# Four edits around the convolutions of a one-core network: who adds up, who splits, when offsets are turned and where group statistics are taken

## The chip, the cores and the metric

The kernel runs on one core of one Trainium2 chip. The metric is the device time of one launch in microseconds (us). Before the change the median of three runs is 1823.61 us (1823.13 to 1826.45).

## The reference

A network of four blocks works on `x` of shape (8, 64, 32, 32) in float32. Every block is `x = x + conv(ln(x))`, then on tokens `t = t + ffn(ln(t))`. The parts that matter here, shortened:

```python
# conv 0: batch norm over all images, then linear attention
mean, var = x.mean(axis=(0, 2, 3)), x.var(axis=(0, 2, 3))
xn = (x - mean) * rsqrt(var + 1e-5) * bn_gamma + bn_beta
k, q, v = wk @ xn + bk, wq @ xn + bq, wv @ xn + bv          # softmax of k over pixels, of q over channels
# conv 1: a 3x3 kernel of its own for each image, mixed out of 8 experts
gap = x.mean((2, 3)); cw = relu(gap @ w1.T) @ w2.T
pooled = x.reshape(b, c, 4, 8, 4, 8).mean((3, 5))            # 16 cells of 8x8 pixels
routing = sigmoid(cw[:, :, None] * (pooled.mean(1).reshape(b, 16) @ w_exp.T)[:, None, :])
combined = einsum('bik,koiuv->boiuv', routing, weight)
# conv 3: deformable convolution, then group norm (32 groups) and relu
offset = conv3x3(x, offset_w) + offset_b                     # 18 offsets a pixel
out = deform_conv(x, offset, deform_w)                       # bilinear samples at 9 shifted places
g = out.reshape(b, 32, -1); out = relu((g - mean(g)) * rsqrt(var(g) + 1e-5) * gamma + beta)
```

The four feed-forward parts are mixtures of experts with the two best experts of each token; the change leaves them alone.

## The kernel before

The activations `x` and their normalised copy `xn` stay in SBUF as 128 partitions (2 halves of the batch times 64 channels) by 4096 columns (4 images of 1024 pixels). The program is a chain of stages: a layer norm, a convolution, a layer norm, a mixture, four times over. Each stage is written by hand as one instruction list for each engine, joined by counting semaphores, so an engine does its instructions in written order and waits where the text says so. Engines run from one stage to the next without a barrier, except around the sampling of conv 3, where a `Block` of its own ends: there all engines meet.

The names that the change touches:

- `split_weights` (GpSimd) cuts the first weights of the next mixture into a rounded part `w_high` (copies, L456) and a rest `w_low` (subtractions, L460), 512 columns at a time; only the next mixture needs them. It is called in conv 0, 1, 2 and in `offsets`.
- `batch_norm` (conv 0): VectorE joins the statistics, TensorE averages the two halves (L1189), VectorE and ScalarE work out scale and shift in operations of one column (L1215 to L1222), and VectorE scales `xn` image by image (L1225, semaphore `bn.scaled`). TensorE multiplies by the key weights (L962) as each image is there. Meanwhile `keep_awake` (L54) gives TensorE products into a bank that nobody reads.
- `conv1`: VectorE sums `xn` in runs of 8 pixels (`row_sum`, L1320), then over 8 rows (`cells`, L1321), then to one total an image (L1323). Small products on TensorE (L1288 to L1291) and a sigmoid give the routing; VectorE mixes one kernel an image (L1337 to L1342), and TensorE convolves (L1301).
- `offsets` (conv 3): TensorE makes the offsets in two rounds `r` of two images each (L1630, 64x32 tiles, 8 at a time side by side), ScalarE adds the bias (`off`, L1616), TensorE turns them (L1638), VectorE copies them to `coords` (L1661) and looks for the largest (L1665 to L1673). The result `flag` says whether any offset leaves the near window.
- `sample_near`: the near samples as a pipeline over items; VectorE multiplies hat weights (`weigh`, L1866), TensorE turns (L1737) and multiplies (L1766) them, `keep` (L1872) takes half an image of results to `y`.
- `sample_rest`: the far samples, all under a condition. Each engine loads `flag` (L1930) and branches (L1931). With these inputs the flag is 0 and the body is skipped. It has a block of its own, so a barrier (L1912) ends it.
- `group_norm`: eight `bn_stats` over `y` (L2118), then a chain of small operations, a product (L2094) and the affine part.

## Time and profile before

| | |
|---|---|
| median of three runs | 1823.61 us |
| time of the profiled execution | 1823.78 us |
| span of its trace | 1822.0 us |
| TensorE busy | 1684.6 us (92%) |
| VectorE busy | 1083.1 us (59%) |
| ScalarE busy | 975.4 us (54%) |
| GpSimd busy | 870.1 us (48%) |
| mean granted clock of TensorE | 0.97 |

The shares are averages over very different stages. The four mixtures fill most of the span and keep TensorE busy; in the pieces between them one engine after the other is alone on the path. In the rows below, the first two numbers of a timeline row are the start and the length in us, PE is TensorE, PEld its weight loads, DVE VectorE, ACT ScalarE, POOL GpSimd, and a name with q at its end is an engine's sequencer.

### The profile page before, as it was taken

The page shows a single profiled execution, that of the slowest core. Times are in us where ns is not written, and L with a number is a line of the kernel's source. Part 1 is how long each engine was busy: PE and PEld are TensorE (multiplying, and loading weights), DVE is VectorE, ACT ScalarE, POOL GpSimd, SP SyncE. Part 2 cuts the span into 40 slices and gives each one's busy share as a digit, 9 for nine tenths or more (in the row PEclk, how much of TensorE's full clock was granted, in tenths as well). Part 3 has the DMA queues.
Part 4 walks back from the last instruction along what each step waited for, and adds up shares of the span by engine and source line. Part 5 has one row for each costly group of instructions (what it writes and reads, how often), then busy time and mean ns, then how long its engine had stood idle before and what let it go on. Part 6 is the DMA issues. An engine that isn't in the chain of part 4 may idle for free. (4 is left out here: it accounts for less than half of the span.)

```text
span 1822.0 us, 32613 instructions
## 1 busy us (share of the span) xinstructions
PE 1684.6 (92%) x12391; PEld 962.3 (53%) x12391; DVE 1083.1 (59%) x1532; ACT 975.4 (54%) x1427; POOL 870.1 (48%) x730
## 2 busy tenths in 40 slices
PE   6879999999589999998999997999999769999998
PEld 3744555555244444444444445777777535555554
DVE  6666777766874342365334236656657467777766
ACT  2444555555336666626666645666666355555554
POOL 3318777777024333313333335333323018777777
PEclk8989999999799999999999998999999889999999
DMA  5004333333302222301222240000000003333333
GB/s 125 1 10 110 107 106 110 107 109 99 91 1 77 89 79 70 88 17 33 90 79 71 88 96 1 2 1 2 1 1 1 3 18 113 110 117 115 113 113 104
DMA packets 71588, 121.64 MB, mean 67 GB/s; under 512 B 16962, under 2 KB 18562, under 8 KB 70786
## 3 DMA queue, kind: packets, MB, share of 16 engines
q1 hardware_dynamic: 71426, 119.47, 23.1%
q8 instruction: 103, 1.69, 0.4%
q14 instruction: 59, 0.48, 0.1%
HBM read 115.74 MB, written 3.67 MB: 66 GB/s over the span
## 5 line engine op out<-in xcount | busy, mean ns | idle before, releaser
L747 POOL TENSOR_TENSOR x<-x,mx_gated 128x512 f32<-128x512 f32 x254 | 327.2, 1288 | 97.4 <-DVE mx_gated L699 96.1
L692 DVE TENSOR_TENSOR mx_hidden<-ps,mx_hidden 128x1024 f32<-128x1024 f32 (+1 forms) x256 | 246.1, 961 | 181.6 <-PE ps L560 181.6
L560 PE MATMUL ps<-tokens_high,w_high 64*128 64x512 f32 x1536 | 331.3, 427 | 13.6 <-DVE mx_hidden L692 6.6
L855 ACT ACTIVATE mx_hidden<-ps,w_bias 128x1024 f32<-128x1024 f32 x256 | 264.2, 1114 | 121.3 <-PE ps L560 121.3
L560 PE MATMUL ps<-tokens_low,w_high 64*128 64x512 f32 x1536 | 306.7, 395 | 0.0
L560 PE MATMUL ps<-tokens_high,w_low 64*128 64x512 f32 x1536 | 306.5, 395 | 0.0
L901 POOL TENSOR_TENSOR x<-x,mx_gated 128x512 f32<-128x512 f32 x126 | 161.4, 1281 | 256.4 <-DVE mx_gated L873 256.4
L873 DVE SCALAR_TENSOR_TENSOR mx_gated<-ps,w_bias,mx_gates 128x512 f32<-128x512 f32 x128 | 96.0, 750 | 283.2 <-PE ps L825 266.3
L675 ACT ACTIVATE mx_hidden<-ps 128x1024 f32<-128x1024 f32 x256 | 248.5, 1022 | 15.9 <-PE ps L560 1.9
L629 PE MATMUL ps<-mx_hidden,w_second 128*64 128x512 f32 x1024 | 249.3, 605 | 4.8 <-DVE mx_hidden L692 3.4
L1866 DVE TENSOR_TENSOR c_near_weights<-c_near_hats 128x768 f32<-128x768 f32 x192 | 190.1, 1037 | 103.3 <-PE ps L1737 103.2
L560 PEld LDWEIGHTS ps<-tokens_high,w_high 64*128 64x128 f32 x1536 | 146.2, 186 | 189.8 <-DVE mx_hidden L692 95.1
L825 PE MATMUL ps<-mx_hidden,w_second 128*64 128x512 f32 x1024 | 233.4, 598 | 0.0
L667 ACT COPY mx_kept<-ps 128x512 f32<-128x512 f32 x126 | 74.0, 587 | 263.0 <-PE ps L560 263.0
L740 POOL TENSOR_TENSOR mx_hidden<-mx_kept,mx_hidden 128x512 f32<-128x512 f32 x126 | 172.6, 1370 | 67.8 <-ACT mx_kept L667 67.8
L699 DVE TENSOR_TENSOR mx_gated<-ps,mx_gates 128x512 f32<-128x512 f32 x256 | 172.3, 685 | 7.0 <-PE ps L629 6.9
L560 PEld LDWEIGHTS ps<-tokens_high,w_low 64*128 64x128 f32 x1536 | 146.1, 186 | 34.4
L560 PEld LDWEIGHTS ps<-tokens_low,w_high 64*128 64x128 f32 x1536 | 146.7, 187 | 23.4
L1844 POOL TENSOR_TENSOR c_near_dist<-c_near_position,c_ints 128x288 f32<-128x288 f32 x64 | 65.1, 1018 | 194.7 <-DVE c_near_hats L1856 191.3
L1815 ACT COPY c_near_matrix<-ps 128x512 f32<-128x512 f32 x288 | 149.1, 608 | 8.5 <-PE ps L1737 8.4
L1737 PE MATMUL ps<-identity,c_near_weights 128*128 128x128 f32 x1152 | 138.7, 278 | 0.0
L825 PEld LDWEIGHTS ps<-mx_hidden,w_second 128*64 128x64 f32 x1024 | 68.0, 136 | 133.6 <-issue 115.3
(222 smaller groups left out, 1830.5 us busy)
## 6 DMA issues: line engine op xcount, KB each, us to landing
mx_gates<-gate_board SPq DMA_DIRECT2D x768, 128.0 KB, 3.1
w_first<-in_f_first SPq DMA_DIRECT2D x4, 1024.0 KB, 12.0
c_weight<-in_c_weight SPq DMA_DIRECT2D x1, 2304.0 KB
x<-in_x SPq DMA_DIRECT2D x8, 256.0 KB, 5.3
w_second<-in_f_second SPq DMA_DIRECT2D x4, 512.0 KB, 13.3
w_first<-in_f_first SPq DMA_DIRECT2D x4, 512.0 KB, 10.1
out_x<-x SPq DMA_DIRECT2D x16, 128.0 KB, 2.7
gate_board<-xn SPq DMA_DIRECT2D x16, 64.0 KB, 2.8
```

The source lines that it names most:

```text
L560: last = pe.matmul(out[h], weights[w][half(h), w_own], tokens[t][half(h), t_own], start=(p == 0), stop=(p == 2))
L629: last = pe.matmul(out[half(h), slot(n), :], w.second[:, e * C:(e + 1) * C], hidden[:, n % HIDDEN, h, :], start=True, stop=True)
L675: act.activation(hidden[:, n % HIDDEN], first[:, n % FIRST], ACT.Silu).then_inc(s.act.semaphore, 1)
L692: dve.tensor_tensor(own, second[:, 0:halves, :], own, ALU.mult).then_inc(s.hidden.semaphore, 1)
L699: dve.tensor_tensor(gated[:, n % GATED, :], out[:, slot(n), :], gates.spread[:, n % gates.SLOTS, :], ALU.mult).then_inc(s.gated.semaphore, 1)
L740: pool.tensor_tensor(own, kept[:, m // 2 % KEPT, :], own, ALU.mult).then_inc(s.other.semaphore, 1)
L747: pool.tensor_tensor(place, place, gated[:, n % GATED, :], ALU.add).then_inc(s.added.semaphore, 1)
L825: last = pe.matmul(out[half(h), slot(n), :], w.second[:, (e * F + f) * C:(e * F + f + 1) * C], hidden[:, n % HIDDEN, f, h, :], start=(f == ...
L855: act.activation(hidden[:, n % HIDDEN, f], first[:, (n * F + f) % BLOCKS], ACT.Gelu, bias=w.bias1[:, e * F + f:e * F + f + 1]).then_inc(s. ...
L901: pool.tensor_tensor(place, place, gated[:, n % GATED, :], ALU.add).then_inc(s.added.semaphore, 1)
L1815: act.copy(own, turned[:, c % BANKS, :].rearrange("p (h b c) -> p h b c", h=HALVES, c=P)).then_inc(s.matrix, 1)
L1866: dve.tensor_tensor(weights[:, u % SLOTS].rearrange("p t (r c) -> p t r c", c=W), spread(own[:, :, W:W + ROWS], 3, W), spread(own[:, :, 0: ...
```

## The change

1. `split_weights` takes a function that is called between its two loops; in conv 0 it waits until all four images are scaled, so that the subtractions come behind the batch norm. `keep_awake` there does 2 products, not 4.
2. In conv 1 GpSimd sums the cells of the first two images (`ON_GPSIMD`) by halving, in six additions an image; VectorE sums the other two and then waits for GpSimd's. `keep_awake` with 12 products is new behind the small products.
3. In `offsets` the first round's offsets are turned amid the second round's products, and their largest and smallest are found before the second round's.
4. The `bn_stats` of the group norm move into `sample_near`, two places behind each `keep`. Each engine loads `flag` there too. The body of `sample_rest` and the group norm stand in one block, so the barrier between them is gone; where the far samples are taken, the statistics are taken again.

```diff
-def split_weights(k, pool):
+def split_weights(k, pool, between=None):
...
         pool.tensor_copy(w.high[:, own], w.first[:, own]).then_inc(k.gt.w_high, 1)
+    if between:
+        between()
     for own in pieces:
...
-            split_weights(k, pool)
+            split_weights(k, pool, lambda: pool.wait_ge(k.bn.scaled, IMAGES))
...
-        keep_awake(k, pe, awake, 4)
+        keep_awake(k, pe, awake, 2)
...
             pool.memset(padded[:], 0.0).then_inc(s.cleared, 1)
+            for j in range(ON_GPSIMD):
+                pool.wait_ge(k.ln.normed, normed + 2 * (j + 1))
+                folded = pixels_of(j, j + 1)
+                for i, width in enumerate((CELL // 2, CELL // 4, CELL // 8)):
+                    to = partial[:, i, 0:H * POOL * width] if width > 1 else rows_of(j, j + 1)
+                    to = to.rearrange("p (n x) -> p n x", x=width)
+                    pool.tensor_tensor(to, folded[:, :, 0:width], folded[:, :, width:2 * width],
+                                       ALU.add).then_inc(s.pool_rows, 1)
+                    pool.wait_ge(s.pool_rows, 5 * j + i + 1)
+                    folded = to
...
+                for i, height in enumerate((CELL // 2, CELL // 4, CELL // 8)):
...
+                    pool.tensor_tensor(to, folded[:, :, 0:height, :], folded[:, :, height:2 * height, :],
+                                       ALU.add).then_inc(s.pool_cells if height == 1 else s.pool_rows, 1)
...
             pe.matmul(tiny[:, 64:128], average[:], cells[:], start=True, stop=True).then_inc(s.small_ps, 1)
+            keep_awake(k, pe, ps[0][:, 0, :], 12)
...
-            done(dve.tensor_reduce(row_sum[:], xn[:].rearrange("p (n x) -> p n x", x=CELL), AX.X, ALU.add))
-            done(dve.tensor_reduce(cells[:].rearrange("p (j q) -> p j q", q=POOL),
-                                   row_sum[:].rearrange("p (j y q) -> p j q y", y=CELL, q=POOL), AX.X, ALU.add))
+            done(dve.tensor_reduce(rows_of(ON_GPSIMD, IMAGES), pixels_of(ON_GPSIMD, IMAGES), AX.X, ALU.add))
+            done(dve.tensor_reduce(cells_of(ON_GPSIMD, IMAGES), cell_rows_of(ON_GPSIMD, IMAGES), AX.X, ALU.add))
+            dve.wait_ge(s.pool_cells, ON_GPSIMD)
...
+        TURN_AT = 4
...
                 for t in range(TAPS):
+                    if r == 1 and t in (TURN_AT, TURN_AT + 1):
+                        turn(0, t - TURN_AT)
...
-            dve.tensor_reduce(reach[:, 0:1], rows, AX.XY, ALU.max)
-            done(dve.tensor_reduce(reach[:, 1:2], rows, AX.XY, ALU.min))
-            dve.scalar_tensor_tensor(out=reach[:, 2:3], in0=reach[:, 1:2], scalar=-1.0, in1=reach[:, 0:1],
-                                     op0=ALU.mult, op1=ALU.max).then_inc(s.reach, 1)
+            done(dve.scalar_tensor_tensor(out=reach[:, 4:6], in0=reach[:, 2:4], scalar=-1.0, in1=reach[:, 0:2],
+                                          op0=ALU.mult, op1=ALU.max))
+            dve.tensor_tensor(reach[:, 6:7], reach[:, 4:5], reach[:, 5:6], ALU.max).then_inc(s.reach, 1)
...
+                if g == 1 and ty == 6:
+                    statistics(j, 0)
+                if g == 1 and ty == 1 and j >= 1:
+                    statistics(j - 1, 1)
                 for h in range(HALVES):
                     weigh(n, h)
...
+            look(dve)
             keep(IMAGES - 1, 1)
-            dve.wait_ge(s.kept, 2 * IMAGES)
+            statistics(IMAGES - 1, 1)
+            dve.wait_ge(s.stats, 2 * IMAGES)
...
-        block = ctx.enter_context(nc.Block(no_gpsimd_drain=True))
+        block = k.block
...
-            for g in range(N // BANK):
-                last = dve.bn_stats(stats[:, g, :], y[:, g * BANK:(g + 1) * BANK])
-            done(last)
```

Three places in the built program show what moves. First GpSimd in conv 0, with the semaphores that each instruction waits for: the copies and subtractions of `split_weights`, then the softmax of the queries. Before:

```order
6 L456 CAST w_high<-w_first 128x512 [waits w_loaded]
7 L456 CAST w_high<-w_first 128x512 x7
8 L460 ISA
9 L460 TENSOR_TENSOR w_low<-w_first,w_high 128x512 [waits gt_w_high] x8
10 L1040 TENSOR_TENSOR c_qv<-c_qv,c_q_max 128x8x128 [waits c0_q_max] x4
```

and of the change:

```order
6 L456 CAST w_high<-w_first 128x512 [waits w_loaded]
7 L456 CAST w_high<-w_first 128x512 x7
8 L462 ISA
9 L462 TENSOR_TENSOR w_low<-w_first,w_high 128x512 [waits gt_w_high,bn_scaled]
10 L462 TENSOR_TENSOR w_low<-w_first,w_high 128x512 [waits gt_w_high] x7
11 L1042 TENSOR_TENSOR c_qv<-c_qv,c_q_max 128x8x128 [waits c0_q_max] x4
```

The order is the same; the first subtraction now also waits for `bn_scaled`. Second, TensorE in `offsets`, the products of the offset convolution and the transposes of `off`. Before:

```order
1844 L1630 MATMUL ps<-c_padded,c_w_off 32x512 x144
1845 L1638 MATMUL ps<-identity,c_off 128x128 x16
1846 L1642 MATMUL ps<-identity,c_reach 1x128
```

and of the change:

```order
1845 L1676 MATMUL ps<-c_padded,c_w_off 32x512 x104
1846 L1661 MATMUL ps<-identity,c_off 128x128 x4
1847 L1676 MATMUL ps<-c_padded,c_w_off 32x512 x8
1848 L1661 MATMUL ps<-identity,c_off 128x128 x4
1849 L1676 MATMUL ps<-c_padded,c_w_off 32x512 x32
1850 L1661 MATMUL ps<-identity,c_off 128x128 x8
1851 L1683 MATMUL ps<-identity,c_reach 1x128
```

Eight of the sixteen transposes now stand between products, in two groups of four. Third, VectorE at the end of the sampling: the last multiplications of weights, the last `keep` and the way to the group norm. Before:

```order
787 L1866 TENSOR_TENSOR c_near_weights<-c_near_hats 128x768 x8
788 L1872 COPY c_y<-ps 128x512
789 L1686 UNCONDITIONAL_BRANCH
790 L2014 UNCONDITIONAL_BRANCH
791 L2075 MEMSET c_rest_staged 128x96 x2
792 L1930 TENSOR_LOAD c_flag
793 L1930 ISA x2
794 L1931 COMPARE_AND_BRANCH
```

and of the change:

```order
798 L1918 TENSOR_TENSOR c_near_weights<-c_near_hats 128x768 x8
799 L1746 TENSOR_LOAD c_flag
800 L1746 ISA x2
801 L1924 COPY c_y<-ps 128x512
802 L1929 BN_STATS c_stats<-c_y 128x6
803 L1730 UNCONDITIONAL_BRANCH
804 L2079 UNCONDITIONAL_BRANCH
805 L1991 COMPARE_AND_BRANCH
```

The load of the flag moved ahead of the last copy, one of the statistics stands behind it, and the clearing of the staging buffer left the way to the branch.

## Rows read from the trace of the kernel before

**Rows 1.** The page's costliest groups: busy, mean ns, idle before and its releaser.

```profile
L1866 DVE TENSOR_TENSOR c_near_weights<-c_near_hats 128x768 f32<-128x768 f32 x192 | 190.1, 1037 | 103.3 <-PE ps L1737 103.2
```

**Rows 2.** Timeline of the batch norm (start, length, engine, line, idle before).

```profile
32.40 3.76 PE L54 MATMUL ps<-identity 128*128 128x256 f32 x8
...
33.05 11.62 POOL L460 TENSOR_TENSOR w_low<-w_first,w_high 128x512 fp32r<-128x512 f32 x8
...
33.58 0.75 DVE L1220 TENSOR_TENSOR bn_both<-bn_both,c_cols 128x1 f32<-128x1 f32 x1
...
36.81 6.74 DVE L1225 TENSOR_SCALAR xn<-xn,bn_both 128x1024 f32<-128x1024 f32 x4
38.58 0.50 PEld L962 LDWEIGHTS ps<-xn,c_wk 128*128 128x128 f32 x2 [3.13 <-DVE xn L1225]
...
56.20 1.91 POOL L1040 TENSOR_TENSOR c_qv<-c_qv,c_q_max 128x1024 f32<-128x1024 f32 x1 [11.53 <-DVE c_q_max L1113]
```

**Rows 3.** Timelines elsewhere: two like operations of VectorE with GpSimd idle.

```profile
1458.83 0.16 DVE L2134 TENSOR_TENSOR gn_group<-gn_group 128x4 f32<-128x4 f32 x1
...
481.49 0.52 DVE L1337 TENSOR_SCALAR c_mixed<-c_weight,c_routing 128x576 f32<-128x576 f32 x1 [0.30 <-ACT c_routing L1281]
```

**Rows 4.** Windows (length, busy PE PEld DVE ACT POOL, granted clock, DMA) as the clock rises.

```profile
41.00:42.00 1.00, 1.00 (x2) 0.29 (x1) 1.00 (x2) 0.38 (x1) 1.00 (x2) 0.56 0.00 0
...
492.00:493.00 1.00, 1.00 (x12) 0.30 (x8) 0.96 (x2) 0.00 (x0) 0.00 (x0) 0.78 0.00 0
```

**Rows 5.** Timeline of conv 1.

```profile
462.83 1.28 DVE L159 TENSOR_TENSOR xn<-xn,ps 128x512 f32<-128x512 f32 x2 [0.74 <-ACT xn L131]
...
471.66 4.42 DVE L1320 TENSOR_REDUCE c_row_sum<-xn 128x512 f32<-128x4096 f32 x1
476.11 1.06 DVE L1321 TENSOR_REDUCE c_cells<-c_row_sum 128x64 f32<-128x512 f32 x1
...
478.58 0.69 PE L1291 MATMUL ps<-c_cells,c_average 128*128 128x64 f32 x2
...
488.14 33.24 PE L1301 MATMUL ps<-c_padded,c_kernel 64*64 64x512 f32 x288 [8.87 <-DVE c_kernel L1342]
...
509.27 0.82 DVE L1342 SCALAR_TENSOR_TENSOR c_kernel<-c_weight,c_routing,c_mixed 128x576 f32<-128x576 f32 x1
```

**Rows 6.** GpSimd's two-input operations: page (busy, mean ns) and timeline.

```profile
L747 POOL TENSOR_TENSOR x<-x,mx_gated 128x512 f32<-128x512 f32 x254 | 327.2, 1288 | 97.4 <-DVE mx_gated L699 96.1
...
1171.43 0.32 POOL L1846 TENSOR_TENSOR c_near_dist<-c_near_position,c_ints 128x72 f32<-128x72 f32 x1
```

**Rows 7.** Timeline of `offsets`: the transposes and what follows.

```profile
1094.60 1.30 PEld L1638 LDWEIGHTS ps<-identity,c_off 128*128 128x128 f32 x12 [0.84 <-issue]
...
1097.25 0.75 DVE L1665 TENSOR_REDUCE c_reach<-c_coords 128x1 f32<-128x576 f32 x1
```

**Rows 8.** Timeline of the sampling behind an image's end.

```profile
1206.97 2.29 DVE L1866 TENSOR_TENSOR c_near_weights<-c_near_hats 128x768 f32<-128x768 f32 x2
...
1208.12 2.84 PE L1737 MATMUL ps<-identity,c_near_weights 128*128 128x128 f32 x24
```

**Rows 9.** From the sampling to the group norm: timeline, and sequencer rows by line.

```profile
1444.15 0.69 DVE L1872 COPY c_y<-ps 128x512 f32<-128x512 f32 x1 [11.95 <-PE ps L1766]
...
L1686 PEldq EVENT_SEMAPHORE  x2: 51/51/51, 1444.4 to 1445.3; - x2
...
L1931 PEldq COMPARE_BRANCH  x1: 4090/4090/4090, 1446.3 to 1446.3; - x1
L1931 DVEq COMPARE_BRANCH  x1: 67/67/67, 1446.8 to 1446.8; - x1
...
L1912 DVEq DRAIN  x1: 74/74/74, 1450.0 to 1450.0; - x1
...
1450.96 4.84 DVE L2118 BATCH_NORM_STATS2 gn_stats<-c_y 128x6 f32<-128x512 f32 x8 [4.87 <-PEq L1912]
...
1456.79 0.60 PE L2094 MATMUL ps<-gn_own,c_pairs 128*128 128x8 f32 x2 [12.70 <-DVE gn_own L2126]
```

More of the change, by code:

```diff
@@ L1240, in conv1 @@
     RING = 3
+    ON_GPSIMD = 2
     with ExitStack() as ctx:
@@ L1616, in _, with turn @@
                     act.activation(off[:, r, h, :], ps[r][:, h, :], ACT.Identity, bias=off_b).then_inc(s.off, 1)
+        TURN_AT = 4
         @block.tensor
         def _(pe):
+            def turn(r, h):
+                pe.wait_ge(s.off, HALVES * r + h + 1)
+                for q in range(CHUNK_TILES):
+                    last = pe.transpose(turned[:, r, h, q * P:(q + 1) * P], off[:, r, h, q * P:(q + 1) * P], k.identity[:])
+                last.then_inc(s.turned, 1)
             pe.wait_ge(k.fetched_sem, k.fetched)
@@ L1697, in sample_near, with look @@
         block = ctx.enter_context(nc.Block(no_gpsimd_drain=True))
+        beyond = {}
+        def look(eng):
+            beyond[eng.engine] = eng.value_load(flag[0:1, 0:1], min_val=0, max_val=1)
         def place_of(n):
@@ L1922, in sample_rest, with run @@
         turned, sum_ps = banks(k, 0, 2, TAP_GROUP), banks(k, 2 * TAP_GROUP, 2)
[L1923 to L1927 removed]
+        block = k.block
+        def run(eng, body, prepare=None, conclude=None):
+            with eng.If(beyond[eng.engine] > 0):
+                if prepare:
+                    prepare()
                 with eng.Fori(0, IMAGES, 1) as j:
                     body(j)
[L1930 to L1932 removed]
+                if conclude:
+                    conclude()
         @block.tensor
```

81 lines of the change are left out of this document (54 added, 27 removed).

## The prediction, made before the changed kernel ran

> **What bounds the kernel now.** I read the page first. By the table above TensorE is busy for 92% of the span and VectorE for 59%, so no engine but TensorE can be the bound of the whole. But the change touches none of the mixtures that fill most of that time. It touches four pieces between them, and there the share says nothing: I took the timeline of each piece and asked which operation the next engine's first instruction waits for. In the batch norm it is VectorE's scaling (TensorE's weight load for L962 waited 3.13 us for L1225) [rows 2]. In conv 1 it is VectorE's sums and then its first kernel (8.87 us of TensorE's idle time) [rows 5]. In `offsets` it is TensorE's products and then VectorE's search. At the end of the sampling it is first TensorE, then the branches and the barrier, then VectorE's statistics (L2094 waited 12.70 us) [rows 9]. Inside the sampling TensorE is the pace: VectorE's weights waited 103.2 us for its transposes [rows 1]. All pieces stand one behind another, so what one gains or loses reaches the end. The sum is made against the profiled execution's own 1823.78 us, which is 0.17 us above the median of the three runs.
>
> **1, batch norm: -3.6 us.** VectorE's three one-column operations from L1220 on take from 33.58 to 36.81, 3.23 us, while GpSimd subtracts for 11.62 us beside them [rows 2]. The like operation L2134, with GpSimd idle, took 0.16 us [rows 3], 0.20 with the gap to the next. Three make 0.6, saving 2.6. The first scaling ran from 36.81 until TensorE loaded at 38.58, 1.77 us, and the four took 6.74 [rows 2]. Undisturbed, L1337 with the same operation does 576 columns in 0.52 [rows 3]; scaled to 1024 that is at most 0.92, and with a fixed part of some 0.2 it is 0.77. I take 0.77, saving 1.0; the bound is 0.85. TensorE's key products then start at 35.0. The reduced `keep_awake` makes room for that: eight half-products took 3.76 us [rows 2], so two products end at 34.3; four would end at 36.2 and eat 1.2 of the gain. What moves is hidden: the subtractions start when the fourth image is scaled (35.0 + 3 x 0.7 = 37.1), take 8 x 1.29 by the row of a like size [rows 6] and end at 47.4. GpSimd's next work, L1040, started at 56.20 after 11.53 us of waiting for VectorE [rows 2] and would now start at 52.6, so the cover is 5 us; beyond it each us late is one us on the queries. The copies stay where they are. If GpSimd was not what slowed VectorE, the gain is 0. The unlike lengths of like operations speak against that.
>
> **2, conv 1: -4.85 us.** VectorE's sums of 4.42 and 1.06 us are halved [rows 5]: 2.7 less. For GpSimd I draw a line through 512 columns in 1.29 us and 72 in 0.32 [rows 6]: 0.16 fixed and 0.0022 a column. An image takes 512, 256, 128, 64, 32 and 16 columns: 6 x 0.16 + 1008 x 0.0022 = 3.2 us, and five waits for its own results at 0.1, a guess, give 3.7. The first image is normalised at 464.1 (462.83 + 1.28), so two end at 471.5. VectorE reaches its wait at 471.66 + 2.2 + 0.5 = 474.4 [rows 5]. GpSimd has 2.9 us of room, and may take 5.1 an image.
>
> Against this stands a rule of the Trainium skill (Perfetto Trace Analysis, section Optimizing Scalar/DVE Operations): VectorE and GpSimd share an SBUF read port, so moving work between them might not help. The skill's SBUF — State Buffer, section Who interferes with whom, narrows it: on this chip a reduction never contends, nor does an ordinary operation with one SBUF input, and VectorE's here are of these kinds. The trace shows contention for the two kinds that page names, L1220 with two SBUF inputs and the scaling [rows 2]; it has no reduction of VectorE beside a running GpSimd in conv 1.
>
> The filler products come on TensorE behind L1291, which ended at 479.27 and now ends at 476.6. The first kernel, needed for L1301, comes at 488.14 - 2.7 = 485.4, so they have 8.8 us. At 3.76 / 4 = 0.94 us each they would take 11.3 at the low clock [rows 2]. But the clock rises from its lower level (1.2 GHz) to the upper (2.4 GHz) under work: in the batch norm 3.3 us after L962 began, in conv 1 4.3 us after L1301 began (granted 0.56 and 0.78 in the windows where it rose) [rows 4]. With 4.3 us at the low rate, 4.6 products, and 7.4 at 0.47, the filler takes 7.8 us and ends in time. L1301 then runs at the upper level from its start; its first 4.3 us were at half rate, so 2.15 are saved of 33.24. What remains is 31.1, 7.8 an image. VectorE must keep ahead with the kernels: the last one was there at 510.09 [rows 5], now 507.4, and is needed at 485.4 + 3 x 7.8 = 508.7. That holds, with 1.3 to spare.
>
> **3, offsets: +0.9 us.** This part I expect to lose. TensorE's products set the pace until ScalarE's last bias. The eight transposes of the first round were hidden before: they ran while ScalarE evicted the second. Amid the products they cost their own time: weight loads of twelve take 1.30 [rows 7], so eight 0.87. Each of two changes from the tiled products to whole-array transposes may add a drain: TensorE's loads stood idle 0.84 us ahead of the first transpose, but half of this is the length of the last products themselves [rows 7]. I take 0.15 each, 1.2 in all; the bounds are 0.9 and 2.6 (2 x 0.84 more). VectorE's copies of the second round end as far behind the products as before, since they wait for the same ScalarE and TensorE work. The two reductions over 576 elements, 0.75 each [rows 7], become two over half: with some 0.2 fixed, 0.5 each, so 0.5 less. One more small operation costs 0.2. Net -0.3 against +1.2.
>
> **4, statistics in the sampling: +1.3 us.** Seven `bn_stats` of 0.6 (4.84 / 8) [rows 9], nearly 0.7 with their wait, come into VectorE's list. VectorE waits 103.3 us for TensorE in all there, over 190.1 us of work [rows 1], so a place takes 0.7 for nothing unless it stands in a tight stretch. Those behind the middle of an image I cost at nothing by that. Behind the end of an image the stretch is tight: the weights of L1866 are done at 1209.26, and the second of the two sets that TensorE turns from 1208.12 on is wanted halfway through those 2.84 us, at 1209.54 [rows 8]. With 0.7 more VectorE is 0.4 late there, and TensorE pays it at three image ends. Bounds: 0, and 7 x 0.7 = 4.9.
>
> **4, the way to the group norm: -6.3 us.** Before: the last copy ends at 1444.84, all engines meet and are released at 1445.3, TensorE reaches its branch at 1446.3, which holds it for 4.09 us, VectorE has its branch at 1446.8 and is through at 1450.0, the second barrier opens, statistics start at 1450.96, and L2094 at 1456.79 [rows 9]. After: one `bn_stats` and its wait move the release to 1446.0. There are no flag loads or memsets ahead of the branches. The stall of the branch stays; I have no row that would shorten it. The Trainium skill (Runtime: NRT & Kernel Launch, Instruction fetch mechanics) says that a taken branch to a far target must fetch its page first, which agrees with 4.09 us here. TensorE is through at 1446.1 + 4.1 = 1450.2. VectorE branches at some 1446.3, needs 3.2 and then the small operations from 1455.80 to 1456.79, 1.0: 1450.5. So L2094 starts at 1450.5, 6.3 earlier. Bounds: 5, if a fetch is one us longer, and 7.
>
> **Sum.** -3.6 - 4.85 + 0.9 + 1.3 - 6.3 = -12.6. 1823.78 - 12.6 = 1811.2 for an execution like the profiled one, 1811.0 as a median.
>
> **Rivals.**
> - *The clock in the batch norm rises later.* Before, 3.76 us of filler had not raised it, and now the cover is half as long [rows 2, 4]. If the key products run at the lower level for some 4 us longer, at most half of that is lost: +2. The same in conv 1: if it does not rise under the filler, that ends at 487.9, 2.5 late, and L1301 gains little. Times 1813 to 1815.5. For it: the risings at 3.3 and 4.3 us differ already. The skill's TensorE: Matmul & The Clock Gate, Part 1, has the clock follow recent activity, which is this mechanism. Chance 0.15.
> - *VectorE has no room in the sampling.* All seven statistics cost TensorE 0.7: 1814.8. Against it: the 103.3 us of waiting [rows 1]. Chance 0.1.
> - *Sharing between VectorE and GpSimd helps nothing in conv 1*, by the rule above: the 2.7 fall away, 1813.9. Chance 0.07.
> - *The branch eats the barrier's gain.* Only the statistics' 4.84 less 0.7 are won, not the rest: -4.1, 1813.4. Chance 0.1.
> - *GpSimd's folds are late: slower.* Their inner runs are 4, 2 and 1 elements. L1846 with nine runs took 0.32 [rows 6]; all of it put on the runs, 0.035 each, makes 412 runs an image 14.6 us. Beyond 5.1 an image each further us costs two. From 11.4 on the whole change loses; at 14.6 the time is 1811.2 + 19 = 1830. Against it: L1040 with 32 runs takes 1.91 for twice the columns of L747 in one run [rows 2, 6], so runs cost about nothing. Chance 0.03.
> - *Within 0.2%.* Two or three of the first four together, and the upper bound of the transposes. Chance 0.04.
> - The forecast itself, 0.51.
>
> **How the numbers follow.** 0.2% is 3.6 us, about what a measurement of this kernel can tell from no change. The forecast and the first four rivals are all faster by more: 0.93. Same 0.04, slower 0.03. The range goes down to 1807.5 (0.2 and 0.7 more in parts 1 and 4, no loss in the sampling, 0.3 less in the offsets, and a clock that rises a us or two earlier) and up to 1816.5 (two of the rivals at once).
>
> **What would show it.** Right: the three one-column operations under 0.3 us each, the first scaling under 0.9; key products from 35.0; GpSimd's last fold before 472.0 on the old scale; the convolution's products in under 31.5 us; the group's product less than 6 us behind the last `keep`. Wrong: a wait of VectorE for `pool_cells`; TensorE's filler ending behind the first kernel; transposes amid the products with gaps over 0.5 us; TensorE waiting for weights behind each image's end.

## The result, and the profile after

The changed kernel takes 1812.62 us (median of four runs, 1810.42 to 1815.48) against 1823.86 (1823.13 to 1826.45): ratio 0.9937, 95% interval 0.992 to 0.9954. The forecast was 1811.0 (1807.5 to 1816.5). The profiled execution took 1815.48, the slowest of the four, over a span of 1813.7. So its trace is 8.3 us shorter than the one of before (1822.0), while the medians lie 11.2 apart, and the stages have to say where that comes from.

The page of the changed kernel: TensorE's share, the granted clock by slices, and the row that answers to [rows 1].

```profile
PE 1693.6 (93%) x12411; PEld 968.2 (53%) x12411; DVE 1071.0 (59%) x1533; ACT 975.3 (54%) x1427; POOL 870.0 (48%) x742
...
PEclk8889999999899999999999998999999979999999
...
L1918 DVE TENSOR_TENSOR c_near_weights<-c_near_hats 128x768 f32<-128x768 f32 x192 | 188.3, 1028 | 101.8 <-PE ps L1786 101.8
```

VectorE waits as long for TensorE in the sampling as before, less 1.5 us. TensorE is busy for 9.0 us more in a span 8.3 shorter. This isn't more time at the lower clock: the trace of before has 111.0 us at granted 0.50, this one 101.3. It is mostly the new filler: from VectorE's first sum to the end of conv 1's products TensorE is busy for 40.6 us in place of 34.7, and behind the group's product for another 3.1 more; the other stages nearly cancel.

Batch norm, timeline of the changed kernel, to be held against [rows 2].

```profile
33.19 0.50 PEld L1191 LDWEIGHTS ps<-bn_own,c_halves 128*128 128x128 f32 x2 [7.35 <-DVE bn_own L1214]
...
33.64 2.05 PE L54 MATMUL ps<-identity 128*128 128x256 f32 x4
...
34.79 0.16 DVE L1222 TENSOR_TENSOR bn_both<-bn_both,c_cols 128x1 f32<-128x1 f32 x1
...
35.38 2.98 DVE L1227 TENSOR_SCALAR xn<-xn,bn_both 128x1024 f32<-128x1024 f32 x4
36.24 0.50 PEld L964 LDWEIGHTS ps<-xn,c_wk 128*128 128x128 f32 x2 [1.27 <-DVE xn L1227]
```

The small operation is down from 0.75 to 0.16 us, four scalings from 6.74 to 2.98. The load of the key products comes 3.05 us behind that of the norm's own product. What moved is hidden, as forecast: the subtractions end at 48.29, and GpSimd's next work starts at 54.01, after 5.72 us of waiting for VectorE.

Conv 1, timeline: GpSimd's second image, VectorE's sums, the filler and the products ([rows 5]).

```profile
465.64 1.28 POOL L1290 TENSOR_TENSOR c_partial<-xn 128x512 f32<-128x512 f32 x1
...
468.90 0.22 POOL L1298 TENSOR_TENSOR c_cells<-c_partial 128x16 f32<-128x16 f32 x1
469.52 2.29 DVE L1356 TENSOR_REDUCE c_row_sum<-xn 128x256 f32<-128x2048 f32 x1
471.84 0.60 DVE L1357 TENSOR_REDUCE c_cells<-c_row_sum 128x32 f32<-128x256 f32 x1
472.48 0.22 DVE L1359 TENSOR_REDUCE c_total<-c_cells 128x4 f32<-128x64 f32 x1
...
474.33 8.27 PE L54 MATMUL ps<-identity 128*128 128x256 f32 x24
483.42 1.09 PE L1337 MATMUL ps<-c_padded,c_kernel 64*64 64x512 f32 x8 [0.81 <-DVE c_kernel L1378]
```

GpSimd is through at 469.12, before VectorE begins, and the total shows no wait. The filler ends at 482.60 and the kernel is what the product waits for.

Offsets, timeline: TensorE's second round with both insertions, and what follows.

```profile
1082.73 1.95 PE L1676 MATMUL ps<-c_padded,c_w_off 64*32 64x512 f32 x31
...
1084.62 0.66 PE L1661 MATMUL ps<-identity,c_off 128*128 128x128 f32 x4
...
1085.20 1.09 PE L1676 MATMUL ps<-c_padded,c_w_off 64*32 64x512 f32 x16
...
1086.22 0.66 PE L1661 MATMUL ps<-identity,c_off 128*128 128x128 f32 x4
...
1090.58 1.26 ACT L1652 ACTIVATE c_off<-ps,c_cols 128x512 f32<-128x512 f32 x2 [7.91 <-PE ps L1676]
...
1094.34 0.27 PE L1683 MATMUL ps<-identity,c_reach 128*1 128x128 f32 x1 [1.79 <-DVE c_reach L1712]
```

Sampling behind an image's end ([rows 8], 4.88 us earlier here): the statistic, the two sets of weights with a hat between them, TensorE's turning.

```profile
1199.38 0.69 DVE L1929 BATCH_NORM_STATS2 c_stats<-c_y 128x6 f32<-128x512 f32 x1
1199.54 0.68 POOL L1895 TENSOR_TENSOR c_near_dist<-c_near_position,c_ints 128x288 f32<-128x288 f32 x1 [11.82 <-DVE c_near_hats L1908]
1199.98 2.04 DVE L1918 TENSOR_TENSOR c_near_weights<-c_near_hats 128x768 f32<-128x768 f32 x2
...
1201.95 0.34 DVE L1908 TENSOR_SCALAR c_near_hats<-c_near_dist 128x360 f32<-128x360 f32 x1
1202.20 2.30 DVE L1918 TENSOR_TENSOR c_near_weights<-c_near_hats 128x768 f32<-128x768 f32 x2
...
1203.23 2.85 PE L1786 MATMUL ps<-identity,c_near_weights 128*128 128x128 f32 x24
```

The kernel before at the same place, with no statistic:

```profile
1204.36 2.31 DVE L1866 TENSOR_TENSOR c_near_weights<-c_near_hats 128x768 f32<-128x768 f32 x2
1204.43 1.43 POOL L1844 TENSOR_TENSOR c_near_dist<-c_near_position,c_ints 128x288 f32<-128x288 f32 x1 [11.81 <-DVE c_near_hats L1856]
...
1206.59 0.46 DVE L1856 TENSOR_SCALAR c_near_hats<-c_near_dist 128x360 f32<-128x360 f32 x1
```

From the sampling to the group norm ([rows 9]), timeline:

```profile
1439.58 0.69 DVE L1924 COPY c_y<-ps 128x512 f32<-128x512 f32 x1 [11.95 <-PE ps L1815]
1440.31 0.69 DVE L1929 BATCH_NORM_STATS2 c_stats<-c_y 128x6 f32<-128x512 f32 x1
1445.10 0.42 DVE L2190 BATCH_NORM_AGGREGATE gn_own<-c_stats 128x2 f32<-128x12 f32 x4 [4.09 <-issue]
...
1446.05 0.60 PE L2166 MATMUL ps<-gn_own,c_pairs 128*128 128x8 f32 x2 [6.51 <-DVE gn_own L2195]
```

The sequencer's row of the branch, by line:

```profile
L1991 PEldq COMPARE_BRANCH  x1: 3835/3835/3835, 1441.7 to 1441.7; - x1
```

TensorE is through its branch at 1445.5, and the product waits for VectorE (`gn_own`). VectorE's own branch ends at 1441.67, and its next operation starts at 1445.10, 3.43 us later, with no wait that the profile shows.

One table holds all fourteen traces, so that the experiments can be read by stage. Each figure is the difference of two times in the timeline, starts unless an end is named. Batch norm: own product to key product. Conv 1: VectorE's first sum to the end of the convolution's products. R1: the offsets' first product to ScalarE's first bias. R2+: from there to the sampling's first instruction. Near: to the last `keep`. Tail: to the group norm's product. End: the next layer norm's first product to the span's end. Us is the median of all runs.

```
kernel         us       b.norm  conv1   R1     R2+    near    tail   end
before         1823.86  6.62    49.72   9.02   13.15  343.92  12.64  360.16
changed        1812.62  3.05    45.03  10.12   14.27  343.91   6.47  362.60
turns_behind   1812.42  3.07    45.02   9.84   13.28  344.29   6.63  363.76
own_block      1810.09  3.08    45.02  10.05   14.36  343.93   7.10  360.70
stats_behind   1815.43  3.07    45.02   9.11   14.26  344.15  10.87  361.12
no_bn_wait     1814.47  7.28    45.02   8.40   14.26  344.45   6.67  362.77
no_filler      1812.00  3.06    47.67   8.99   14.40  343.91   6.81  361.06
gn_filler      1806.88  3.04    45.02   9.10   14.26  344.33   6.76  359.02
awake4         1811.40  4.00    45.02   8.13   14.35  343.92   6.51  360.89
one_turn       1810.63  3.05    44.98   9.38   13.95  344.18   6.79  362.42
best           1805.71  3.08    45.02   9.11   13.27  343.43   6.76  360.70
before_filler  1822.01  6.73    48.99   9.52   13.53  344.02  13.81  359.07
gpsimd3        1811.94  3.08    45.23   8.13   14.24  344.63   6.53  359.82
gn_filler2     1811.22  3.08    45.02  10.12   14.26  344.55   6.79  362.89
```

What the change's own places gave, after less before: -3.57, -4.69, +1.12, 0.0 and -6.17, together -13.3. Against the second trace of the old structure (before_filler, which differs in TensorE's list behind the group's product alone) the same places give -3.68, -3.96, +0.74, -0.1 and -7.34, together -14.3: a stage of one trace is good to about 1 us. The rest of the trace of after is 5.0 longer: the program's start 1.24 (the batch norm's product at 33.19, before 31.96, ahead of all that the change touches), R1 1.10, the end 2.44, and 0.25 between. In the variants, whose instructions are the same at these places, R1 is 8.1 to 10.1 and the end, where no four fillers were added, 359.8 to 363.8.

### The profile page after: what moved, and what is told of

The parts are those of the page before. It is cut to its first block and busy times, and to the rows that moved or that the text cites. A ratio compares the mean times of both kernels' runs of the same rounds, so it can differ in the third digit from the quotient of the medians.

```text
span 1813.7 us, 32654 instructions
## 1 busy us (share of the span) xinstructions
PE 1693.6 (93%) x12411; PEld 968.2 (53%) x12411; DVE 1071.0 (59%) x1533; ACT 975.3 (54%) x1427; POOL 870.0 (48%) x742
## 5 line engine op out<-in xcount | busy, mean ns | idle before, releaser
L1895 POOL TENSOR_TENSOR c_near_dist<-c_near_position,c_ints 128x288 f32<-128x288 f32 x64 | 60.9, 951 | 201.3 <-DVE c_near_hats L1908 195.6
## 6 DMA issues: line engine op xcount, KB each, us to landing
w_second<-in_f_second SPq DMA_DIRECT2D x4, 512.0 KB, 13.9
```

## The experiments

Each group of four kernels was run beside the kernel before, whose median there was 1825.65 us for the first four of the table below the changed kernel, 1828.01 for the next four and 1825.09 for the last. Single runs of one kernel lie up to 9 us apart, so effects of one or two us are read from the stages.

**turns_behind.** The first round's transposes behind the products again.

```diff
-                    if r == 1 and t in (TURN_AT, TURN_AT + 1):
-                        turn(0, t - TURN_AT)
...
-            for h in range(HALVES):
-                turn(1, h)
+            for r in range(ROUNDS):
+                for h in range(HALVES):
+                    turn(r, h)
```

> The changed kernel with the four times two transposes of the first round put back behind the products of the second; the search stays in two halves. In the changed kernel the second round took 9.18 us from ScalarE's first bias of one round to that of the next, before 7.66. Theory: the transposes and the two changes to and from the tiled products cost TensorE 1.5 us there, and hiding VectorE's copies of the first round gave back nothing; this kernel's second round takes 7.7 and its way from the last product to the sampling's first instruction 3.8 to 4.3, so offsets is 1.1 to 1.5 us shorter and the whole 1811.2 to 1811.6 against 1812.6. Rival: the copies and half the search of the first round, now behind the products, cost as much there: the way behind the products is 5.3 or more and the whole is unchanged. A gap of 1.4 us of TensorE in the first round, ahead of the transposes, where before it was 0.8 a little later, should be gone (round one 10.1 again) if it comes from the transposes, and stay if it comes from where the code lies.

R2+ fell from 14.27 to 13.28, and 1.0 us is what the insertion loses; it is just under the expected 1.1. The second round took 7.67 (1080.20 to 1087.87), as before.

```profile
1087.87 1.27 ACT L1652 ACTIVATE c_off<-ps,c_cols 128x512 f32<-128x512 f32 x2 [6.40 <-PE ps L1674]
...
1092.16 0.27 PE L1682 MATMUL ps<-identity,c_reach 128*1 128x128 f32 x1 [2.32 <-DVE c_reach L1711]
```

The way from the second round's first bias to the product with `reach` is 4.29, against 3.76 in the changed kernel and 4.17 before: VectorE's hidden copies and half search are worth 0.5, and the search in halves by itself nothing. R1 stayed long (9.84), so its gap is not the transposes'. The whole (1812.42, ratio 0.9922, 0.9901 to 0.9943) cannot tell 1 us.

**own_block.** `block = ctx.enter_context(nc.Block(...))` in `sample_rest` in place of `k.block`, and `open_part(k)` behind it.

> The changed kernel with the old block of its own round the rare branches of the sampling, so the engines meet once more between these and the group norm; the statistics stay in the sampling. Theory of the prediction: of the 6.2 us won from the last image's end to the group's product the statistics are 4.1 and the rest is the second meeting, the loads of the flag and the memsets, of which this edit brings back the meeting alone: the group's product comes 7.0 to 8.0 us behind the last keep instead of 6.5, the whole 1813 to 1814. Rival: the branch's fetch and the meeting overlap entirely, and the time is that of the changed kernel, 6.5 us; other rival: the second meeting costs a fetch on each engine again, 9 us or more.

The tail is 7.10: the second meeting costs 0.3 to 0.6 beside the tails of 6.47 to 6.81, at the foot of the expected range. In the ten traces without the meeting and with the statistics in the sampling, the tail is VectorE's pause behind its own branch (3.43 to 3.77 us) plus 3.04; TensorE's branch (3.44 to 3.90) doesn't enter it. With the meeting it does, and of the twelve traces of the new structure this one has the shortest branch, so a longer one would have cost more (not tried). The whole, 1810.09, is below the changed kernel's median; its end of 360.70 is 1.9 shorter in the trace, so the stage decides. VectorE waited for TensorE's sequencer at the meeting (timeline), whose branch had stalled for 3.43 us:

```profile
1440.29 0.43 DVE L2190 BATCH_NORM_AGGREGATE gn_own<-c_stats 128x2 f32<-128x12 f32 x4 [4.72 <-PEq L1976]
```

**stats_behind.** All eight `bn_stats` in the group norm again, without the meeting.

```diff
-                if g == 1 and ty == 6:
-                    statistics(j, 0)
-                if g == 1 and ty == 1 and j >= 1:
-                    statistics(j - 1, 1)
...
+            for g in range(N // BANK):
+                last = dve.bn_stats(stats[:, g, :], y[:, g * BANK:(g + 1) * BANK])
+            done(last)
```

> The changed kernel with all eight statistics back in the group norm, as before; no meeting between. Theory: the 4.84 us of statistics come after VectorE's branch and lie whole on the path, less the 0.69 of the one that stands behind the last keep now: the group's product comes 6.5 + 4.1 = 10.6 us behind the last keep, and the sampling's own length stays at 343.9 us, since the seven statistics there cost TensorE nothing (0.0 us measured). Whole: 1816.7 against 1812.6. Rival: the sampling does pay for them in another run (1.3 us as predicted, up to 4.9), then the sampling is shorter here by that and the whole 1815.4 or less.

```profile
1437.76 0.69 DVE L1924 COPY c_y<-ps 128x512 f32<-128x512 f32 x1 [11.95 <-PE ps L1815]
1442.79 4.85 DVE L2180 BATCH_NORM_STATS2 c_stats<-c_y 128x6 f32<-128x512 f32 x8 [4.34 <-issue]
```

Tail 10.87, 4.1 to 4.4 longer than those of 6.47 to 6.81, and the sampling no shorter (344.15). In the three traces without statistics there the sampling took 343.9 to 344.2, in the eleven with them 343.4 to 344.6, so what they cost TensorE is lost in a spread of 1 us. The whole is 1815.43, 2.8 above the changed kernel's; 4.1 was expected.

**no_bn_wait.** `split_weights(k, pool)` in the first convolution without the wait in between.

> The changed kernel in which GpSimd's splitting does not wait for the batch norm's scaling: it subtracts beside VectorE again; keep_awake stays at two. Theory: VectorE is slowed by sharing with GpSimd, so the three small operations take 0.8 to 1.2 us each again in place of 0.16 and the first scaling 1.7 in place of 0.86; the key products start 3.5 to 3.6 us later behind the batch norm's own product, the whole 1816.2. Rival: the shorter filler is what let VectorE's result be used earlier: then the gain stays at 1.2 us or more, and the whole is 1815.0 or less.

```profile
33.38 9.48 POOL L462 TENSOR_TENSOR w_low<-w_first,w_high 128x512 fp32r<-128x512 f32 x7
...
35.91 1.18 DVE L1223 TENSOR_TENSOR bn_both<-bn_both 128x1 f32<-128x1 f32 x1
37.13 1.18 DVE L1224 TENSOR_TENSOR bn_both<-c_cols,bn_both 128x1 f32<-128x1 f32 x1
```

With GpSimd's subtractions beside it VectorE takes 1.18 us for one column and the stage 7.28. The wait is worth all of the gain, and the rival falls: the shorter filler alone gave nothing. The stage is even 0.7 longer than before, since the subtractions now also lie beside an earlier small operation (L1218 took 1.00, its like before 0.24), so the worth of the wait is 3.6 to 4.2 us by where they fall. The whole was 1814.47, 1.9 above the changed kernel's, where 3.6 was expected.

**awake4.** `keep_awake(k, pe, awake, 4)` in the batch norm.

> The changed kernel with four filler products in the batch norm, as before, in place of two. Theory of the prediction: VectorE's way is now 3.05 us long behind the batch norm's own product and the fillers of 3.76 us stand in front of the key products, which start 4.2 to 4.3 us behind it, 1.2 us later; the key products' own time is unchanged, since neither filler raises the clock before they start: the whole 1813.8. Rival (clock): the two fillers more bring the rise forward by what they cost, the key products take 8.2 to 8.6 in place of 9.4 us, and the whole is unchanged.

```profile
32.25 3.76 PE L54 MATMUL ps<-identity 128*128 128x256 f32 x8
35.80 8.56 PE L964 MATMUL ps<-xn,c_wk 128*128 128x512 f32 x16
```

The key products start 0.95 later than in the changed kernel and take 8.56 in place of 9.45 us. From the norm's product to their end it is 12.56 against 12.50: the rival holds, and the shorter filler was worth nothing. The nine other traces with two products and the wait took 12.35 to 13.60 for this way, so a gain or loss under 1 us can't be told from one trace.

**no_filler.** The changed kernel without `keep_awake(k, pe, ps[0][:, 0, :], 12)` in conv 1.

> The changed kernel without the twelve filler products in conv 1; GpSimd's sums stay. Theory of the prediction: the filler only brings the clock up ahead of the convolution's products, and ends in time. Without it the first product starts at the same distance behind VectorE's sums (13.9 us), begins at the lower level and the four images' products take 33.2 us again instead of 31.1: the whole 2.1 us longer, 1814.7. Rival: the clock is still up from the work ahead of the sums, or it falls again in the 0.8 us between filler and products: then nothing changes, 31.1. Rival that ends on the other side: the filler itself holds TensorE's first product up, and 13.9 becomes 13.1.

Windows (columns as in [rows 4]) of four us from the first product of no_filler:

```profile
478.27:482.27 4.00, 4.00 (x20) 1.39 (x24) 3.82 (x6) 0.00 (x0) 0.00 (x0) 0.50 0.00 0
482.27:486.27 4.00, 4.00 (x36) 1.48 (x32) 3.86 (x6) 0.00 (x0) 0.00 (x0) 0.83 0.02 4
```

and of the changed kernel, the filler's two and the first of the products:

```profile
474.33:478.33 4.00, 4.00 (x11) 3.19 (x12) 3.28 (x7) 1.97 (x4) 0.00 (x0) 0.50 0.00 0
478.33:482.33 4.00, 4.00 (x16) 3.28 (x14) 3.86 (x5) 0.00 (x0) 0.00 (x0) 0.77 0.00 0
483.42:487.42 4.00, 4.00 (x40) 1.78 (x44) 3.83 (x6) 0.00 (x0) 0.00 (x0) 1.00 0.01 4
```

The filler takes the low stretch on itself, and the products run 40 to a window where they ran 20. Without it the stage is 2.64 longer (47.67), 33.78 of it the products, where 2.1 was expected. In the two traces of the old structure, also without this filler, the products took 33.24 and 32.52, so it is worth 1.4 to 2.6 us, by how late the clock would have risen. The whole doesn't show it: 1812.00 against the changed kernel's 1812.62, where 1814.7 was expected. The first product stands 13.9 behind the sums in both, so the filler holds nothing up.

**one_turn.** Both halves turned ahead of the fifth tap.

> The changed kernel with both groups of four transposes in one place, ahead of the fifth tap of the second round, in place of one ahead of the fifth and one ahead of the sixth. Measured: two insertions lengthen the round by 1.51 us, of which the transposes of each, from first to the next product, are 0.59 us, so 0.17 an insertion is the change between the kinds of product. Theory: with one change less the round takes 9.18 - 0.17 = 9.0 us. Rival: the extra is in the transposes themselves (each of the eight costs 0.19), then 9.18 stays. Other rival: ScalarE's second bias, 0.9 us behind the first, is now waited for and the round gets longer than 9.2. The whole changes by less than a run can tell; the trace decides.

The round takes 8.87. One change of kind less saves 0.31, more than expected. With two insertions costing 1.51 and one 1.20, the eight transposes cost 0.89 and each insertion 0.31, if the two costs simply add up.

**gpsimd3.** `ON_GPSIMD = 3`.

> The changed kernel with the sums of three images on GpSimd in place of two, one on VectorE. An image took GpSimd 3.5 us, and the second ended 0.4 us before VectorE began its sums. Theory: the third is folded from 469.1 to 472.6 on the scale of the changed kernel's trace, while VectorE, with half as much, is through at 469.5 + 1.15 + 0.35 = 471.0 and waits 1.6 us: its total comes at 472.8 in place of 472.5, so the first product stands 14.1 us behind VectorE's first sum in place of 13.9, and the whole is unchanged. Rival (the shared port): GpSimd's folds beside a reducing VectorE take longer than 3.5 us or stretch the reduction over 1.2 us; then 14.6 or more.

```profile
465.20 1.22 DVE L1356 TENSOR_REDUCE c_row_sum<-xn 128x128 f32<-128x1024 f32 x1
...
468.36 0.22 DVE L1359 TENSOR_REDUCE c_total<-c_cells 128x4 f32<-128x64 f32 x1 [1.52 <-POOL c_cells L1298]
```

VectorE waits 1.52 us for GpSimd and the products start 14.09 behind the first sum, both as expected. Two images of four is where the engines meet. A 1024-element sum took 1.22 beside a running GpSimd; a line through the sums taken alone, 2048 elements in 2.29 and 4096 in 4.42 [rows 5], gives 1.22 too (an estimate). The Trainium skill (SBUF — State Buffer, section Who interferes with whom) says that a reduction doesn't contend, and the trace agrees.

**gn_filler** and **gn_filler2.** Four, and two, fillers behind the group's product of the changed kernel.

```diff
             pe.matmul(mean_ps, pairs[:], own[:, :, 0:2], start=True, stop=True).then_inc(s.group, 1)
+            keep_awake(k, pe, following.mean[:, 0, :], 4)
```

> The changed kernel with four filler products on TensorE right behind the group norm's small product (to the first bank of the next layer norm, which overwrites it). TensorE had 5.05 us of waiting there, less 0.6 for its own product; at the lower level four take 3.76 us (their rate in the batch norm), so they fit with 0.7 to spare. In five traces of the changed kernel and its variants the way from the layer norm's first product to its first variances took 4.9 to 5.4 us and the granted clock was 0.5 until 8.3 to 10 us behind the group's product. Theory: the clock rises under steady work, so it comes up 3 to 4 us earlier, and the layer norm's way shortens to 3.2 to 4.2 us: 1 to 2 us off the whole, 1811 to 1811.6 against 1812.6. Rival, as in the batch norm: the filler stops short of the rise, the 0.7 us of idling undoes it, and the clock rises where it did; no change. It may also move the later fall of the clock (24 us behind the product in three traces), which is worth 1 to 2 us either way.

> The changed kernel with two filler products behind the group norm's small product in place of four: 1.85 us of work, then 2.6 us of idling before the layer norm's first product. Theory: as in the batch norm, where fillers of 2 and 4 products followed by idling left the clock down until the key products had run for 3.3 us, the clock stays down and rises 8.4 to 11 us behind the product, as without filler; from the layer norm's first product to the variances 4.4 to 5.4 us, the whole 1812.6. Rival: any work in the pause brings the rise forward by about its own length: 6.5 to 8 us behind the product, and half of the four products' gain.

Windows of gn_filler, of four us from the group's product:

```profile
1441.73:1445.73 4.00, 4.00 (x10) 2.95 (x10) 1.52 (x8) 1.79 (x3) 0.00 (x0) 0.51 0.00 0
1445.73:1449.73 4.00, 2.99 (x7) 1.06 (x6) 4.00 (x4) 4.00 (x6) 0.00 (x0) 1.00 0.00 0
```

and those of the changed kernel where the clock falls again, 24 us behind the product:

```profile
1466.05:1470.05 4.00, 2.20 (x42) 1.59 (x40) 3.33 (x5) 2.92 (x7) 0.36 (x1) 0.99 0.00 0
1470.05:1474.05 4.00, 3.67 (x27) 2.30 (x27) 0.62 (x2) 1.69 (x5) 2.17 (x2) 0.50 0.00 0
```

With four the clock is up (read from half-us windows, as all such distances here) 4 us behind the product, the way to the variances takes 3.20 us (5.36 in the changed kernel), and the end is 359.0, the shortest of all fourteen. The whole is 1806.88, below the three that ran beside it (1810.6 to 1812.0), which is more than the 1.9 to 3.4 us by which its end is shorter than theirs; the rest is not explained. With two it rose 11 us behind and fell again at 24.7, and the end is 362.9: no gain, as expected.

**before_filler.** The same four in the kernel before.

> The kernel before with four filler products behind the group norm's small product, and nothing else. Theory: the late clock of the layer norm is not a thing of the change; the kernel before had 5.05 us of waiting there and the lower clock until 8.4 us behind the product too. So the rise comes at about 4 us, the way from the layer norm's first product to its variances takes 3.2 us in place of 4.44, and the layer norm's first product to the end takes 359 us in place of 360.2 (with other falls of the clock in between, 358 to 361). Rival: the filler helps only the changed kernel, whose TensorE comes out of a shorter pause; then 4.4 and 360 stay. It is also a second trace of the old structure: it tells how far the round of the offsets' first products (9.02 us before, 8.1 to 10.1 since) and the stretch from the key products to conv 1 (433.1 before, 428.8 to 433.3 since) vary without the change.

The way to the variances is 3.19 and the end 359.07; the whole is 1822.01 against 1825.09, ratio 0.9985 (0.9975 to 0.9995), for a line that has nothing to do with the change. The medians lie 3.1 us apart; the end of the two traces accounts for 1.1 of it. As a second trace of the old structure it has R1 of 9.52, 428.3 from the key product to conv 1's sums, where the first had 433.1, and a tail of 13.81 (12.64 before), in which TensorE's branch took 1.0 us longer than the 4.09 of [rows 9]:

```profile
L1931 PEldq COMPARE_BRANCH  x1: 5089/5089/5089, 1444.6 to 1444.6; - x1
```

**best.** turns_behind, gn_filler, and four fillers behind the sampling's first value product.

```diff
-            for v in range(G):
+            value(0)
+            keep_awake(k, pe, acc[:, 0, :], 4)
+            for v in range(1, G):
```

> Three edits on the changed kernel, each with a place of its own in the trace. The first round's transposes go behind the products of the second (round two and the way behind them 13.3 us in place of 14.3). Four filler products follow the group norm's small product, 5 us of waiting that four of them fill (the clock up at 4 us behind it in place of 8.4 to 11.0 us; from the layer norm's first product to its variances 3.2 us in place of 4.9 to 5.4). And four more stand behind the sampling's first value product, where TensorE idles 4.6 us and then turns the first two sets of weights in 5.08 us at the lower clock, against 2.84 later. Theory: the clock is up by then, the first turning takes 3 us, and the sampling is 1.5 to 2 us shorter than 343.9 to 344.5. The whole: 1806.9 of the group norm's filler alone, less 1.0 and 1.7: 1804.2. Rival: the sampling's pace at its start is VectorE's weights, so it stays at 343.9 and the whole is 1805.9; it could be longer if the filler is still running when the second value product is free to start (4.56 us of room, 3.7 needed).

```profile
1099.50 4.09 PE L1785 MATMUL ps<-identity,c_near_weights 128*128 128x128 f32 x24
```

The median is 1805.71 (1803.13 to 1810.47; ratio 0.9898, 0.988 to 0.9917), 5.5 and 6.2 under the variants gn_filler2 and gpsimd3 that ran beside it. Its ratio to the kernel before lies below the changed kernel's 0.9937 (0.992 to 0.9954) without overlap; the two were not run side by side. Two of its three parts did less than expected. In the sampling the clock, up 7.8 us behind the sampling's start, was down again from 11.2 to 14.6. The first turning took 4.09, against 4.1 to 5.4 in the thirteen traces without this filler, and the stage is 0.5 shorter than the shortest of them. Behind the group's product the same four fillers did not bring the clock up in this profiled run:

```profile
1437.66:1441.66 4.00, 4.00 (x10) 2.95 (x10) 1.53 (x8) 1.80 (x3) 0.00 (x0) 0.50 0.00 0
1441.66:1445.66 4.00, 3.16 (x5) 1.41 (x5) 4.00 (x4) 3.75 (x5) 0.00 (x0) 0.50 0.00 0
```

It rose at 9.2, against 4.0 in the two other traces with four; in the eleven traces without four it rose at 8.0 to 11.0. So a filler of 3.7 us can bring the rise forward, and not every run gets the gain.

## Why the prediction was right

The time is 1.6 us above the forecast, and the terms, summed with the stages' own figures, give -13.3 against -12.6. In part this closeness is luck. The statistics were mis-sized by 1.3 us and the other terms by 0.5 together the other way, and the medians differ by 11.2, less than the stages gave, since the rest of the trace grew for reasons that the prediction did not have.

*Batch norm, -3.6: -3.57.* The mechanism was right: VectorE was slowed by GpSimd's subtractions, shown by no_bn_wait. The scaling took 0.86 against 0.77, and the key products start at 35.0 on the scale of before, as forecast. One side remark failed, "four would end at 36.2 and eat 1.2 of the gain". They delay the start by 0.95, and in the one trace (awake4) the earlier rise of the clock returns it.

*Conv 1, -4.85: -4.69.* The sums gave 2.58 of 2.7, the clock 2.10 of 2.15. GpSimd took 3.46 to 3.48 us an image against 3.7. The filler took 8.27 against 7.8 and still ended 0.8 ahead of the kernel. The caution that moving work between VectorE and GpSimd might not help (the Trainium skill, Perfetto Trace Analysis, section Optimizing Scalar/DVE Operations) did not come true here: GpSimd's sums were through 0.4 us before VectorE began its own, and the 2.58 came off the path.

*Offsets, +0.9: +1.12.* Transposes amid products cost 1.51 in place of 1.2. The term that was mis-sized is the change between kinds of product, 0.31 an insertion where 0.15 was taken (by one_turn); the eight loads were 0.89 against 0.87. Behind the products 0.41 came back, 0.3 was forecast. turns_behind shows the loss at the end of it, 1.0.

*Statistics in the sampling, +1.3: 0.0.* The step that failed is "With 0.7 more VectorE is 0.4 late there". In the trace of after the statistic takes 0.69, but the second set of weights ends at 1202.20 + 2.30 = 1204.50, which on the scale of before is 1209.38, against 1209.26 [rows 8]: 0.12 later. So the set was still 0.16 ahead of the 1209.54 at which it was wanted. The rest of the 0.7 is covered by shorter work of VectorE: the weights behind the statistic took 2.04 where the like set took 2.31, and the hat between the sets 0.34 for 0.46. GpSimd ran its two-input subtractions beside the weights before; now it does part of them beside the statistic. That sharing is the cause is argued from these rows and not tested by a run. That TensorE pays nothing for the statistics is shown within the spread of the sampling's length, 1 us: stats_behind is no shorter there.

*Way to the group norm, -6.3: -6.17.* The product came at 1450.6 on the scale of before (1450.5 was forecast), and VectorE's way was the last to end, as forecast. The statistics are 4.1 to 4.4 of it (stats_behind), the second meeting 0.3 to 0.6 (own_block); the remainder, the flag's load and the memsets, was not tried alone. TensorE's branch still stalled for 3.84 us, but nothing waited for it. Against the second trace of the old structure the gain is 7.34, beyond the bound of 7, since there TensorE's branch, which the barrier waits for, took 5.09 in place of 4.09.

*The rivals.* In conv 1 the clock came up under the filler and in the batch norm 3.6 us into the key products, as forecast. In own_block it rose only 6.1 us into them, and they took 10.53 us in place of 9.45: the first rival, which cost 1.1 there and isn't excluded for other runs. Where the profiled run lost 2.4 us was a place that the prediction did not look at, the layer norm behind the group norm: the clock rose 10.3 us behind the group's product (8.4 before) and fell again at 24. The change doesn't make this necessary: gpsimd3 has all its edits, and there the clock rose at 8.0 and the end took 359.8; with the filler both structures reach 359. But the nine other traces of the new structure without four fillers rose at 9.4 to 11.0. Whether the shorter tail makes the late rise likelier stays open: there is one trace of the old structure without a filler there. The other rivals did not come: no wait for `pool_cells`, no pace set by VectorE, no branch that ate the gain.

## What to carry to other kernels

Ask of each wait on the path whether its length is the engine's own or a neighbour's: 0.16 us for one column beside 1.18 shows it at once. Moving the neighbour's work behind it is free if its user is late enough; here 5.7 us were left. Before slipping small work into TensorE's stream, count what it hides against its own time and 0.3 us an insertion; here 0.5 was hidden for 1.5. Look at the granted clock at the first products behind every pause, since some unused products there were worth as much as a careful reordering, though not in every run.

## What the runs showed of the hardware

- A filler helps when the products that matter follow under a clock that it has raised (conv 1: 1.4 to 2.6 us). Where the clock was still at 0.50 when they began, it gave nothing that the stages show: two products in the group norm's pause (the end 362.9 us), four in the batch norm (12.56 us against 12.50).
- Behind the group's product the late rise and the length of the end go together. In the five traces in which the clock rose within 9.2 us, it fell once, 34.7 to 36.5 us behind the product, and the end took 359.0 to 360.7 us. Where it rose at 9.4 to 9.9 (four traces), it fell once more at 30, and the end took 360.7 to 361.1. Where it rose at 10.3 to 11.0 (five traces), that fall came at 24, and the end took 362.4 to 363.8. The instructions there are the same but for the fillers. What sets the time of the rise is not shown.
- The first round of the offsets' products took 8.1 to 10.1 us at full granted clock in the fourteen traces, with the same instructions. In eight of them it is 8.7 us and one gap of TensorE, 0.4 to 1.4 us long, always 3.19 us behind the first product; the profile names no releaser. The cause is open.
- The taken branch held TensorE for 3.4 to 5.1 us in the fourteen traces. VectorE's took 0.06 to 0.07, but its list went on only 3.2 us behind it in the kernel before, 4.3 in before_filler and 3.4 to 3.8 in the others.
